# A two-layer attention and bilinear block: transposes moved to steps 4 and 7, float32 values by VectorE, step 0's exponentials ahead of the last values

## The reference, cut to what matters

```python
# x: (4, 256, 64, 64) float32; _gn is a group normalisation with 32 groups
# layer 0: attention over the 4096 positions, keys and queries of 32 channels, values of 256
f = Wq @ xf + bq; g = Wk @ xf + bk; h = Wv @ xf + bv          # xf = _gn(x) as (B, 256, 4096)
s = einsum('bki,bkj->bij', f, g); beta = softmax(s, axis=1)
x = x + gamma[0] * einsum('bci,bij->bcj', h, beta)
# layer 1: 1x1 convolution to 32 channels, all 528 products of two channels, 1x1 convolution back
y = bn_relu(w1 @ _gn(x)); packed = y[..., rows] * y[..., cols]
x = x + bn_relu(w2 @ packed)
```

## Time and profile before

| | us |
|---|---|
| median of 3 runs | 2166.46 (2166.24 to 2167.27) |
| profiled execution, its own time | 2162.51 |
| span of the profiled execution | 2160.6 |
| TensorE busy | 2088.0 (97% of the span) |
| VectorE busy | 1619.5 (75%) |
| ScalarE busy | 1614.1 (75%) |
| GpSimd busy | 1309.7 (61%) |

### The profile page before, as it was taken

One profiled execution on the slowest core, in us unless ns is written; L12 is line 12 of the kernel. 1 busy time (PEld: TensorE's weight loads), 2 busy tenths in 40 slices (PEclk: granted clock), 3 DMA queues, 4 the chain that ended last, 5 costly groups with the idle time before them and its releaser, 6 DMA issues.

```text
span 2160.6 us, 48571 instructions
## 1 busy us (share of the span) xinstructions
PE 2088.0 (97%) x17838; PEld 1641.9 (76%) x17838; DVE 1619.5 (75%) x3479; ACT 1614.1 (75%) x2594; POOL 1309.7 (61%) x1984
## 2 busy tenths in 40 slices
PE   4799999999999999999999999999999999999999
PEld 2588888888878777777877777777787777777754
DVE  6687877778877777777778777776876767777767
ACT  5577777777777777877777777777877777777767
POOL 3244455556566676776656676666756656566656
PEclk9999999999999999999999999999999999999999
DMA  6044455455456677656477666676635555464532
GB/s 202 21 77 77 75 86 82 85 81 82 84 113 134 142 130 144 133 115 136 73 148 146 115 140 120 142 136 126 127 60 115 110 104 112 93 116 81 112 70 78
DMA packets 592492, 233.62 MB, mean 108 GB/s; under 512 B 541024, under 2 KB 547936, under 8 KB 592224
## 3 DMA queue, kind: packets, MB, share of 16 engines
q1 hardware_dynamic: 592256, 230.53, 55.3%
HBM read 71.83 MB, written 19.92 MB: 42 GB/s over the span
## 4 chain that ended last, share of the span: by engine, by line
PE 85%; DVE 4%; ACT 3%; issue 2%; POOL 2%; SPq 2%; DMA 1%; DVEq 0%; ACTq 0%
PE acc L1749 19%; PE acc L1759 18%; PE acc L1750 18%; PE sps L1574 5%; PE acc L1554 5%; PE tps L1554 5%; PE tps L1625 3%; PE acc L1548 3%; PE tps L1627 2%; PE acc L1625 1%; PE tps L1589 1%; POOL kb L1136 1%; POOL rt L1157 1%; DVE xb L879 1%; ACT ph L1314 1%
## 5 line engine op out<-in xcount | busy, mean ns | idle before, releaser
L1136 POOL TENSOR_TENSOR kb<-ks,kb 128x512 f16<-128x512 f32 x504 | 598.6, 1192 | 447.6 <-DVE kb L860 266.0
L1314 ACT ACTIVATE ph<-sps,esc 128x512 f16<-128x512 f32 x520 | 356.7, 686 | 382.9 <-PE sps L1574 370.8
L1749 PE MATMUL acc<-hth,ph 128*128 128x257 f16 x2080 | 485.2, 274 | 0.0
L1750 PE MATMUL acc<-htl,ph 128*128 128x256 f16 x2080 | 484.8, 273 | 0.0
L1749 PE MATMUL acc<-hth,kt 128*128 128x257 f16 x2016 | 470.7, 274 | 0.0
L1750 PE MATMUL acc<-htl,kt 128*128 128x256 f16 x2016 | 470.1, 273 | 0.0
L1326 ACT ACTIVATE ks<-ks,kbias,esc 128x512 f32<-128x512 f32 x504 | 407.5, 809 | 0.0
L865 DVE TENSOR_TENSOR pl<-sps,ph 128x512 f16<-128x512 f32 x520 | 355.6, 684 | 48.6 <-ACT sps L1315 47.4
L1315 ACT ACTIVATE sps<-sps,esc 128x512 f32<-128x512 f32 x520 | 340.3, 654 | 0.0
L1759 PE MATMUL acc<-hth,pl 128*128 128x257 f16 x2080 | 318.7, 274 | 0.0
L1759 PE MATMUL acc<-hth,kt 128*128 128x257 f16 x2016 | 308.9, 274 | 0.0
(11 more groups left out here) (254 smaller groups left out, 3594.2 us busy)
## 6 DMA issues: line engine op xcount, KB each, us to landing
rt<-turned SPq DMA_DIRECT2D x96, 256.0 KB, 5.0
xt<-x SPq DMA_DIRECT2D x36, 512.0 KB, 4.2
xb<-x SPq DMA_DIRECT2D x32, 512.0 KB, 5.0
out<-zt SPq DMA_DIRECT2D x45, 256.0 KB, 2.8
kt<-kb SPq DMA_TRANSPOSE x504, 3.2
yb<-turned SPq DMA_DIRECT2D x36, 128.0 KB, 2.7
rt<-turned SPq DMA_DIRECT2D x72, 64.0 KB, 2.2
turned<-yb SPq DMA_DIRECT2D x12, 256.0 KB, 2.1
```

Source lines behind the costliest of these rows:

```text
L1136: tt(kb[:, m % KB_RING, 1], ks[:, m % KS_RING], kb[:, m % KB_RING, 0], ALU.subtract).then_inc(kl_ok, 1)
L1314: A(ph[:, v % SLOTS], sps[v % 2][:], ACT.Exp, scale=esc[:]).then_inc(ph_ok, 1)
L1749: mm(bank[:, 0:C + 1], high[:, q], hth[:, c * QT + q], start=(s8 == 0 and q == 0), stop=False)
L1750: mm(bank[:, 0:C], high[:, q], htl[:, c * QT + q], start=False, stop=False)
```

## The change

`BY_ACT` becomes empty, so VectorE writes `xn` for all 8 chunks of the front, and three small VectorE instructions move behind chunk 2. `powers(0)` moves ahead of the last values' `value_high` on ScalarE, `low_part(0)` ahead of the last `value_low` on VectorE, and on TensorE the scores for step 2 move from the head of step 0 to behind its block for the maxima. In every group but a batch's first, the two transposes move from steps 5 and 7 to steps 4 and 7, `finish` from steps 6 and 8 to steps 5 and 8, `second_stats` from steps 7 and 11 to steps 6 and 11.

```diff
-        BY_ACT = [("first", 0, c) for c in range(2, NCH)]
+        BY_ACT = []
...
-                    if part == ("x", 1):
+                    if part == ("x", 2):
                         s(V.tensor_scalar(vout[:], col(K_RV, 2), vc(V_GAMMA), None, ALU.mult))
...
                         c, k = part[1:]
+                        if part == ("v", NCH - 1, 1):
+                            low_part(0)
                         value_low(0, 2 * c + k, c * QT + 2 * k, h_bank(c, k))
...
             def attend(b):
-                if b == 0:
-                    low_part(0)
...
-                        if J and t in (6, 8):
-                            finish(G - 1, (t - 6) // 2, 1)
-                        if J and t in (7, 11):
-                            second_stats(G - 1, (t - 7) // 4, 1)
+                        if J and t in (5, 8):
+                            finish(G - 1, (t - 5) // 3, 1)
+                        if J and t in (6, 11):
+                            second_stats(G - 1, (t - 6) // 5, 1)
...
                         row_copy(0, sps[0])
+                    if part[0] == "scores":
+                        powers(0)
...
-                        if (b == 0 or J or t) and not kept(u):
+                        if (J or t) and not kept(u):
                             powers(u)
...
-                        if u in SCORED:
+                        if u and u in SCORED:
                             scores(SCORED[u])
...
-                        if J and t in (5, 7):
-                            if t == 5 and b and n >= 1:
+                        if J and t in (4, 7):
+                            if t == 4 and b and n >= 1:
                                 pe.wait_ge(y_ok, y_made(n - 1))
-                            if t == 5 and b and n >= 2:
+                            if t == 4 and b and n >= 2:
                                 pe.wait_ge(z_ok, 2 * (n - 1))
...
-                            transposed(G - 1, (t - 5) // 2, 1)
+                            transposed(G - 1, (t - 4) // 3, 1)
...
                         step_piece(u)
+                        if u == 0:
+                            scores(SCORED[u])
                         if not kept(u):
```

More of the change, by code:

```diff
@@ L1724, in attend @@
                             rest_of_z(n - 2)
-                        if J and t in (5, 7):
-                            if t == 5 and b and n >= 1:
+                        if J and t in (4, 7):
+                            if t == 4 and b and n >= 1:
                                 pe.wait_ge(y_ok, y_made(n - 1))
-                            if t == 5 and b and n >= 2:
+                            if t == 4 and b and n >= 2:
                                 pe.wait_ge(z_ok, 2 * (n - 1))
-                            if t == 5 and b < LASTB and 4 <= J <= 7:
+                            if t == 4 and b < LASTB and 4 <= J <= 7:
                                 pe.wait_ge(qk_lo, qk_made(b + 1, 2 * (J - 4)))
-                            if (b, J, t) == (0, 2, 5):
+                            if (b, J, t) == (0, 2, 4):
                                 pe.wait_ge(set_dve, mark["part1"])
-                            transposed(G - 1, (t - 5) // 2, 1)
+                            transposed(G - 1, (t - 4) // 3, 1)
                         if kept(u):
```

## The result

The changed kernel takes 2133.78 us (median of 4 runs, 2132.83 to 2135.18), the kernel before in the same series 2166.86 (4 runs, 2166.24 to 2167.45): ratio 0.9848, 95% interval 0.9831 to 0.9865, or 33.1 us less. The forecast was 2141.0 within 2136 to 2151. The profiled execution has a span of 2133.4 us, an own time of 2135.18 and a mean granted clock of 0.999.

The account below looks back on a forecast made before the run. TensorE, busy 2088.0 of 2160.6 us, was taken as the bound. 18.8 less 0.6, plus 1.5, 3.6 and 2.3, is 25.6 us off 2166.46: forecast 2141, range 2136 to 2151.

Parts of the forecast that it names:

- three of the rivals: Odd groups keep waits, 2154, chance 0.11; half of transposes' gain returns, 2150, 0.10; first transposes wait for ScalarE, 2183, 0.03.
- the fourth: Rival: front's float32 values gain nothing and step 0's clock falls anyway; gain 21.7 us, time 2145, chance 0.11.
- minus 18.8: Term: TensorE's 28 waits of second transposes for VectorE's `finish` all go, saving 18.8 us.
- the term of minus 1.5: Term: slow work after the 1.55 us wait in batch 1's group 1 goes, saving 1.5 us, from 0 to 1.7.
- The estimate of 0.6: Term: 0.6 us given back in group 1 of batch 3, where late VectorE work stays late; between 0 and 2.94.
- The median of the runs shown lies 4 us above that execution, and I put the difference on it.: Step: from the runs' median, 2166.46, the 25.6 us gain was subtracted, giving 2140.9; the profiled execution's own time became 2136.9.
- The front's two terms: Front: float32 values on VectorE save 2.3 us; step 0's earlier exponentials save 3.6 us.
- the 3.6 of step 0: Term: earlier exponentials open step 0 sooner and bring step 3's scores forward, saving 3.6 us, from 2 to 4.0.
- the 2.3 of the values: Term: two `xn` pairs leave ScalarE's path, minus 2.8, plus 0.5 for chunk 0's delay; from 1.3 to 2.8.
- Three marks of the forecast: Signs: chunks 2 and 4 wait near 1.3 us, step 3's scores near 82.3, no half clock appearing elsewhere.
- the best sum of the terms: Largest gain the terms allowed: 18.8 + 1.7 + 4.0 + 2.8, or 27.3 us.

Follow-up runs that it names:

- experiment 3: Kernel before with only `BY_ACT` empty and the three small VectorE instructions behind chunk 2: 2163.41 us against 2166.78, ratio 0.9982, interval 0.9971 to 0.9993.
- experiment 9: Kernel before with second transposes in step 6 and their `finish` in step 7, adding a wait to every group: 2235.74 us against 2167.06, ratio 1.0323.
- experiment 6: Kernel before with only `finish` of half 0 moved to the head of VectorE's step 6, transposes unmoved: 2139.41 us against 2165.88, ratio 0.9878.
- experiment 1: Kernel before, unchanged, run and profiled again: 2165.45 us against 2166.78, ratio 0.9996.
- experiment 4: Kernel before with only `powers(0)`, `low_part(0)` and the scores of step 2 moved: 2163.32 us, ratio 0.9988.
- experiment 2: Kernel before with only the transposes, `finish` and `second_stats` moved: 2140.39 us against 2166.78, ratio 0.9878.
- experiment 8: Changed kernel with `vout`, `gbv` and `idh` back behind chunk 1: 2133.06 us against the kernel before's 2165.88; once more 2133.12 against 2167.06.
- experiment 5: Changed kernel, unchanged, run again: 2135.41 us against the kernel before's 2165.88, ratio 0.9861.

## Why the prediction was right and wrong

**The mechanism** of the transposes was right. The second transposes waited for `finish`, `finish` waited in VectorE's order, and the first transposes have room in step 4. Neither half of the transposes' term came back in the odd groups, nor did a wait for `z_out` or `divide` appear. That refutes three of the rivals; the fourth (the front's values gain nothing, and the clock falls in step 0 all the same) is half refuted: by experiment 3's interval the values do gain something, but the clock's loss may only have moved, since half clock lies in the window 74 to 78 instead of in step 0.

**The step that failed first, a mis-sized term: "minus 18.8".** I took the sum of the brackets. A bracket counts only the time without a running matmul. In the stream the matmuls last 0.27 us and start every 0.11 (the rows at 265.36 and 265.47 in experiment 9), so they overlap by 0.16. Ahead of a wait the last matmul runs to its end with nothing started behind it, and the overlap is lost on top of the bracket. By experiments 6 and 9 (55.72 us a group without a wait, 56.20 with one of 0.30, 57.96 with one of 2.07) that is 0.17 us a wait, and 28 waits make 4.8 us: 23.6 instead of 18.8. (The profile models the ends of matmuls; the price rests on the distances of the groups, and the overlap is the explanation that fits it.)

**The clock.** No run shows the 1.7 us from which the term of minus 1.5 was taken; it was my estimate. In its place the traces of before show 1.6: groups 1 and 2 of batch 1, with a granted clock of 0.50 from 627 to 630, lay 61.90 us apart, those of batch 2, which had the same wait of 1.55 and no half clock (1.00 over 1147 to 1155), 60.31. So the size of the term was right for that profile.

**Given back.** The estimate of 0.6 was close: the changed kernel has one new wait of 0.73 us for the maxima in group 1 of batch 3 (timeline of TensorE below), and one of 1.09 for `ks` in that of batch 1, where 0.66 for `ks` and 0.41 for ScalarE stood before. That is 0.75 more.

```profile
1649.07 0.39 PE L1556 MATMUL tps<-fst,gst 96*128 96x512 f16 x1 [0.73 <-DVE mx L818]
```

**The other step that failed: "The median of the runs shown lies 4 us above that execution, and I put the difference on it."** This took the difference for something that the change leaves alone. I had the median 4.1 us above the own time of the profiled execution (2141.0 and 2136.9); it lies 1.4 below (2133.78 and 2135.18). That makes 5.5 of the 7.2 us between forecast and result. The other 1.7 are the own time itself, 2135.18 instead of 2136.9: 4.5 more from the attention and 2.9 less from the front than forecast. But part of this is the luck of which executions were profiled: nearly the fastest of the kernel before, and the longest of the four of the changed one, which is the whole 1.4.

The traces show where the extra time was. In four executions with the old order (the first profile, experiments 1, 3 and 4) group 1's waits in batches 1 to 3 lie between 1.55 and 3.23 us, and the clock falls in one to three of them; the stretch behind the first second transposes takes 2006.0, 2007.0, 2012.4 and 2005.7 us, 2007.8 on the average. In the six with the new order (the changed kernel three times, experiment 2, and experiment 8 twice) it takes 1981.4 to 1982.7, 1982.0 on the average. So the attention gains 25.7 us, not the 24.2 of two single profiles; the change takes away not only the waits but also what followed from them in some executions. Most of this surplus is one execution, that of experiment 3.

**Term by term,** from the medians of experiments 2, 3 and 4, the account is simpler. The front's two terms were forecast at 2.3 and 3.6 and gave 3.4 and 3.5. The transposes with their clock were forecast at 19.7 and gave 26.4. Of these missing 6.7 us, 4.8 are what the 28 waits cost beyond their brackets, at 0.17 each, so the mis-sized 18.8 is the larger error. An estimate for the rest is 1.8: by so much the first profile's attention (2006.0) lay below the average of the old order (2007.8).

**The front** was forecast to gain 5.9 us. Between TensorE's first keys-and-queries matmul and the first transposes' place in the first group that has them (where they stand in step 5 I take off the 1.77 us of a step), six executions with the old front average 121.7 us (the profile before: 119.4, among the shortest), three with the new one 116.7 (116.4, 117.2 and 116.4): 5.0 us, and by the medians of experiments 3 and 4, 3.4 plus 3.5. Single terms: experiment 4 gave the 3.6 of step 0 (3.5 measured), though some 1.7 of the forecast (half of step 0's 3.3) was the price of half clock in step 0 (1.5 by the traces: the scores of steps 0 and 1 start 3.30 us apart there and 1.77 in experiment 1, at full clock), which in four of seven executions with the old order wasn't there; and experiment 3 the 2.3 of the values within its interval (3.4). `qkl` started at 34.76 where I had said 34.3, of which 0.44 is a later start of the whole front, and chunk 4's wait is 1.31 us as forecast. Three marks of the forecast failed: chunk 2 still waits 2.04 us, step 3's scores start at 86.06, not near 82.3, and half clock appears elsewhere, at 74 to 78.

```profile
47.57 0.60 PE L1556 MATMUL tps<-fst,gst 96*128 96x512 f16 x2 [2.04 <-DMA gst<-qkl]
...
69.68 0.60 PE L1556 MATMUL tps<-fst,gst 96*128 96x512 f16 x2 [1.72 <-DMA gst<-zt]
...
86.06 0.40 PE L1576 MATMUL sps<-gst,fst 128*128 128x128 f16 x4 [0.29 <-DVE pl L865]
```

Behind the first lies one DMA issue that took 1.32 us instead of 0.59 (SyncE's timeline), behind the second a DMA that landed after 3.61 us (the chain that ended last), where the first profile has 2.41. The half clock of the window 74 to 78 comes behind it and behind a wait of 2.4 us for GpSimd's `mrow`.

```profile
43.70 1.32 SPq L438 DMA_DIRECT2D gst<-qkh  x1
```

```profile
66.03 3.61 DMA gst<-zt
```

Neither is an accident of this change. Chunk 2 waits 2.04 to 2.67 us in all four executions with the new list of `xn` (the changed kernel three times, experiment 3), each time behind an issue of 1.3 to 1.8 us instead of 0.59 or a last DMA that landed after 3.41. With the old list it waits 2.38 to 3.92, and only the first profile (2.70) has neither an issue of 1.2 us or more nor a landing of 2.9 or more ahead of it: the forecast of 1.3 started from the one clean case. Chunk 7's last DMA lands after 1.83 (experiment 1) to 3.68 us (experiment 4) with the old list and after 2.70 (experiment 3) to 3.74 (experiment 5) with the new one. These times vary from execution to execution; what causes them isn't settled.

**The range** was too narrow below. Its lower end, 3 us under the best sum of the terms, held nothing for a wait that costs more than its bracket (4.8 us) or for the scatter of the executions.

## What to carry to other kernels

When the engine that bounds a kernel waits for a short instruction, look at what stands ahead of it in its own engine's list; moving that one instruction up gave as much here (26.5 us), within the noise, as moving both sides (26.4). A wait of TensorE cost its bracket and 0.17 to 0.18 us more here, so that 28 waits, 18.8 us by their brackets, were worth some 23.6 by that estimate. Look at the scatter of the runs before a forecast, and profile the kernel twice: where the scatter comes from waits that the change removes, the median falls by more than one fast execution shows: here the attention gained 25.7 us on the average and 24.2 by two single profiles.

## What the hardware showed that I had not expected

- A wait of 0.30 us lengthens a group by 0.48, one of 2.07 by 2.24: 0.17 to 0.18 beyond the idle time.
- The same wait of 1.55 us was followed by half clock (0.50 granted for some 3.4 us) in one batch (distance to the next group 61.90 us) and not in another (60.31). In four executions of the old order the clock fell in one to three of three places.
- The last DMA of chunk 2 landed after 1.83 to 1.85 us in seven of thirteen executions and after 2.91 to 3.41 in the other six.
- In step 0, with nothing changed in its order, TensorE had half clock in three executions (0.51 over 3.30 us in the first profile) and full clock in four (1.00 over 3.30 us in experiment 1); where it was full, the half clock had come earlier in the front (0.58 over 48 to 52 in experiment 6).
- A VectorE instruction on 2 elements a row took 0.22 us between two of GpSimd's instructions and 1.12 beside one.
